# Routed experts as plain fp32 products, and one pass of the shared expert moved to the front

## The reference

```python
probs = softmax(xt @ w_router)                       # 16 experts
top_w, top_i = top_k(probs, 4); top_w = top_w / sum(top_w)
g = silu(einsum('td,edh->teh', xt, we1)) * einsum('td,edh->teh', xt, we3)   # H = 128
moe_out = einsum('teh,ehd->td', g * cw[:, :, None], we2)
shared = silu(xt @ ws1) * (xt @ ws3) @ ws2           # HS = 512
out = shared / 5 + moe_out * 4 / 5
x = x + gb * out
```

## Time and profile before

| | |
|---|---|
| median of 3 runs | 898.1 us (895.02 to 899.46) |
| profiled execution | 898.99 us, span 897.3 us, mean granted TensorE clock 0.917 |
| TensorE products / weight loads | 751.9 us (84%) / 469.8 us (52%) |
| VectorE | 662.9 us (74%) |
| ScalarE | 500.4 us (56%) |
| GpSimd | 268.4 us (30%) |

### The profile page before, as it was taken

How to read it: one execution, slowest core, us unless ns; L and a number is a source line. 1 busy time by engine, 2 the same in 40 slices (tenths; PEclk the granted TensorE clock), 3 DMA queues, 4 the chain that set the end, 5 groups by cost and what they waited for, 6 DMA issues and landing times. The chain is left out here.

```text
span 897.3 us, 15698 instructions
## 1 busy us (share of the span) xinstructions
PE 751.9 (84%) x5208; PEld 469.8 (52%) x5208; DVE 662.9 (74%) x1263; ACT 500.4 (56%) x939; POOL 268.4 (30%) x350
## 2 busy tenths in 40 slices
PE   8479699999999999999998968576788887888574
PEld 7246343444444444444444447465677776777453
DVE  7356888889998999999984377455777777776474
ACT  4221277678777877777776614434557775555111
POOL 7200013233222222233321121750007533420651
PEclk9777699999999999999999877899899998889799
DMA  6756014665544555344500112911337664543431
GB/s 195 183 117 202 18 32 95 180 162 145 148 128 135 154 153 152 82 127 112 133 26 4 50 39 66 333 71 57 109 112 240 220 186 144 159 148 99 145 93 58
DMA packets 78705, 112.37 MB, mean 125 GB/s; under 512 B 15780, under 2 KB 59364, under 8 KB 76516
## 3 DMA queue, kind: packets, MB, share of 16 engines
q1 hardware_dynamic: 68692, 81.67, 32.9%
q0 software_dynamic: 9280, 29.11, 9.5%
q10 hardware_dynamic: 656, 0.59, 0.4%
HBM read 59.92 MB, written 50.99 MB: 124 GB/s over the span
## 5 line engine op out<-in xcount | busy, mean ns | idle before, releaser
L750 ACT ACTIVATE probs<-psum 128x1024 f32<-128x1024 f32 (+3 forms) x384 | 289.8, 816 | 130.5 <-PE psum L935 128.0
L1156 DVE TENSOR_REDUCE max_parts<-psum 128x8 f32<-128x1024 f32 (+2 forms) x192 | 235.3, 1226 | 64.4 <-PE psum L909 60.8
L949 PE MATMUL psum<-probs,v_aug 128*32 128x512 f32 (+3 forms) x1536 | 168.1, 511 | 0.3 <-POOL probs L624 0.3
L935 PE MATMUL psum<-qs,ks 64*128 64x512 f32 (+3 forms) x768 | 157.3, 409 | 5.0 <-ACT probs L750 4.9
L624 POOL TENSOR_SCALAR_AFFINE_SELECT probs<-probs 128x512 f32<-128x512 f32 x128 | 81.6, 637 | 266.9 <-ACT probs L750 266.9
L935 PEld LDWEIGHTS psum<-qs,ks 64*128 64x128 f32 x768 | 73.4, 189 | 130.9 <-ACT probs L750 112.5
L1163 DVE TENSOR_REDUCE max_parts<-psum 128x1 f32<-128x512 f32 x192 | 130.7, 681 | 0.0
L909 PE MATMUL psum<-km,qs 64*128 64x128 f32 (+2 forms) x704 | 93.7, 338 | 34.9 <-DMA km<-k_parts 24.5
L1530 PE MATMUL psum<-w_all,km 128*128 x564 | 104.5, 326 | 10.6 <-issue 8.1
L1530 PEld LDWEIGHTS psum<-w_all,km 128*128 128x128 f32 x564 | 85.0, 214 | 18.8 <-issue 14.6
L1372 POOL DMA_INDIRECT probs<-y_sorted,posi x64 | 62.2, 972 | 106.7 <-DMA y_sorted<-xn 51.8
(11 more groups left out here) (204 smaller groups left out, 1008.7 us busy)
## 6 DMA issues: line engine op xcount, KB each, us to landing
km<-x_sorted SPq DMA_DIRECT2D x94, 128.0 KB, 2.4
y_sorted<-xn SPq DMA_DIRECT2D x94, 128.0 KB
km<-k_parts SPq DMA_DIRECT2D x62, 160.0 KB
x_sorted<-g_rows POOLq DMA_DIRECT2D x6, 1536.0 KB, 10.1
y_sums<-g_sign SPq DMA_DIRECT2D x32, 256.0 KB, 5.2
qs<-q_parts SPq DMA_DIRECT2D x62, 128.0 KB
ks<-k_parts SPq DMA_DIRECT2D x64, 64.0 KB
w_all<-in_L_ffn_we_dram SPq DMA_DIRECT2D x16, 256.0 KB, 6.0
```

The source lines that it names most:

```text
L750: act.activation(probs[s % (LAG + 1)][:, 2 * hh:2 * hh + 2, off:TT], psum[:, 2 * hh:2 * hh + 2, off:TT], ACT.Exp, scale=SCALE).then_inc(p_ ...
L935: last = pe.matmul(bank[2 * hh + hp][:, off:TT], ks[buf][rows, c * P:(c + 1) * P], qs[buf][rows, hh, half * TT + off:(half + 1) * TT], sta ...
L949: last = pe.matmul(bank[sum_bank][32 * h:32 * h + 32, off:TT], v_aug[:, group, c, :], probs[s % (LAG + 1)][:, h, off:TT], start=(c == 0), ...
L1156: dve.tensor_reduce(out=max_parts[:, :, h0:h1, slice(*tiles), slot], in_=psum[:, wide_bank:wide_bank + 2, :].rearrange("p a (s w) -> p (a ...
```

## The change

What it does:

- w_all holds the experts' weights once, as fp32. The splits of weights (ScalarE and VectorE in the lead), of x (VectorE) and of g (ScalarE and VectorE) are gone. A tile has two up products and one down product, in plain fp32.
- VectorE copies the turned g (`turned_out`) and all of y (`products_out`).
- The tile loop is reordered: TensorE up_rows(i), turned_rows(i+2), down_rows(i-2), turned_g(i-1); ScalarE silu(i), shifted_rows(i+2); VectorE product(i), products_out(i-2), turned_out(i-1). SyncE: load(i), store(i-5). up_rows waits for shifted_rows (t_read) instead of split_x.
- NY, the buffers for y, is 4 (3 before), NG, those for gathered rows, 4 (2 before). Tile buffers are their own and no longer parts of km, xn and probs; the first load no longer waits for the first pass.
- LEAD is 3: three passes stand before the tile loop, one behind it, which takes two combinations a step.

```diff
-        w_all = sb(moe, "w_all", [P, E, 2, WCOLS], F32R)
+        w_all = sb(moe, "w_all", [P, E, WCOLS], F32)
...
-        NX, NY, NG = 4, 3, 2
...
+        NX, NY, NG = 4, 4, 4
+        xg, xt = sb(moe, "x_rows", [P, NX, D], F32), sb(moe, "x_turned", [P, 2, D], F32)
+        tm, gt, yt = sb(moe, "tile_mid", [P, 2, P], F32), sb(moe, "tile_g", [P, 2, P], F32), sb(moe, "y_rows", [P, NY, D], F32)
+        acc, rows = sb(moe, "acc", [P, 2, D], F32), sb(moe, "rows", [P, NG, TOPK, D], F32)
...
-        AHEAD_T, BEHIND_Y, STORE_LAG = 3, 2, 8
+        AHEAD_T, STORE_LAG = 2, 5
...
-        LEAD = 2
+        LEAD = 3
...
                     if kk == 0:
                         sp.wait_ge(sorted_s[b], 16 * ROUTES)
-                    if k == 0:
-                        sp.wait_ge(up_full, 2 * NS)
                     if k >= NX:
                         sp.wait_ge(t_full, k - NX + 1)
                     sp.dma_start(xg[:, k % NX, :], xs[b][kk * P:(kk + 1) * P, :]).then_inc(x_in_s[k % NX], 16)
...
-                    if k % 2:
-                        sp.wait_ge(y_act, k // 2 + 1)
-                    else:
-                        sp.wait_ge(y_dve, k // 2 + 1)
+                    sp.wait_ge(y_copied, k + 1)
                     sp.dma_start(ys[b][kk * P:(kk + 1) * P, :], yt[:, k % NY, :]).then_inc(y_out_s[k % NY], 16)
...
-                        if t < 2:
-                            for expert in (2 * q, 2 * q + 1):
-                                act.wait_ge(w_in[expert // 4], 16 * 5)
-                                act.activation(w_all[:, expert, 0, :], w_all[:, expert, 1, :].bitcast(F32), ACT.Copy).then_inc(w_high, 1)
...
-                for i in range(-AHEAD_T, NTILE + BEHIND_Y):
-                    if 0 <= i + 1 < NTILE:
-                        silu(i + 1)
+                for i in range(-AHEAD_T, NTILE):
+                    if i >= 0:
+                        silu(i)
                     if i + AHEAD_T < NTILE:
                         shifted_rows(i + AHEAD_T)
-                    if 0 <= i < NTILE:
-                        high_rows(i)
-                    if i >= BEHIND_Y and (i - BEHIND_Y) % 2:
-                        products_out(i - BEHIND_Y)
...
-                        pe.wait_ge(w_low, E)
-                    pe.wait_ge(x_split, k + 1)
+                        pe.wait_ge(w_in, 16 * 5 * E // 4)
+                    pe.wait_ge(t_read, k + 1)
...
-                    for x, part in ((xh, 0), (xh, 1), (xl, 0)):
-                        for c in range(DC):
-                            last = pe.matmul(bank[U_BANKS[k % 2]][:, 0:2 * H], x[:, k % 2, c * P:(c + 1) * P],
-                                             w_all[:, bass.ds(expert[k], 1), part, c * 2 * H:(c + 1) * 2 * H].rearrange("p a n -> p (a n)"),
-                                             start=(n == 0), stop=(n == 5))
-                            n += 1
+                    for c in range(DC):
+                        last = pe.matmul(bank[U_BANKS[k % 2]][:, 0:2 * H], xt[:, k % 2, c * P:(c + 1) * P],
+                                         w_all[:, bass.ds(expert[k], 1), c * 2 * H:(c + 1) * 2 * H].rearrange("p a n -> p (a n)"),
+                                         start=(c == 0), stop=(c == DC - 1))
...
-                    pe.wait_ge(g_low, k + 1)
...
+                    pe.wait_ge(g_read, k + 1)
+                    if k >= 2:
+                        pe.wait_ge(y_copied, k - 1)
                     else:
-                        pe.wait_ge(y_dve, k // 2)
-                    for n, (g, part) in enumerate(((th, 0), (tl, 0), (th, 1))):
-                        last = pe.matmul(bank[Y_BANKS[k % 2]][:, 0:D], g[:, k % 2, :],
-                                         w_all[:, bass.ds(expert[k], 1), part, W13:WCOLS].rearrange("p a n -> p (a n)"),
-                                         start=(n == 0), stop=(n == 2))
-                    last.then_inc(y_full, 1)
+                        pe.wait_ge(shared_read, 2 * LEAD)
+                    pe.matmul(bank[Y_BANKS[k % 2]][:, 0:D], gt[:, k % 2, :],
+                              w_all[:, bass.ds(expert[k], 1), W13:WCOLS].rearrange("p a n -> p (a n)"),
+                              start=True, stop=True).then_inc(y_full, 1)
...
-                for i in range(-AHEAD_T, NTILE + BEHIND_Y):
-                    if 0 <= i + 1 < NTILE:
-                        up_rows(i + 1)
+                for i in range(-AHEAD_T, NTILE + 2):
+                    if 0 <= i < NTILE:
+                        up_rows(i)
                     if i + AHEAD_T < NTILE:
                         turned_rows(i + AHEAD_T)
-                    if i >= BEHIND_Y:
-                        down_rows(i - BEHIND_Y)
-                    if 0 <= i < NTILE:
-                        turned_g(i)
+                    if i >= 2:
+                        down_rows(i - 2)
+                    if 1 <= i <= NTILE:
+                        turned_g(i - 1)
...
-                        if t < 2:
-                            for expert in (2 * q, 2 * q + 1):
-                                dve.wait_ge(w_high, expert + 1)
-                                dve.tensor_tensor(out=w_all[:, expert, 1, :], in0=w_all[:, expert, 1, :].bitcast(F32),
-                                                  in1=w_all[:, expert, 0, :].bitcast(F32), op=ALU.subtract).then_inc(w_low, 1)
-                        elif t >= LEAD:
+                        if t >= LEAD:
...
-                def low_rows(k):
-                    dve.wait_ge(g_high, k + 1)
-                    dve.tensor_tensor(out=tl[:, k % 2, :], in0=bank[G_BANK][:, 0:P], in1=th[:, k % 2, :].bitcast(F32),
-                                      op=ALU.subtract).then_inc(g_low, 1)
+                def turned_out(k):
+                    dve.wait_ge(g_full, k + 1)
+                    if k >= 2:
+                        dve.wait_ge(y_full, k - 1)
+                    dve.tensor_copy(gt[:, k % 2, :], bank[G_BANK][:, 0:P]).then_inc(g_read, 1)
...
+                for i in range(NTILE + 2):
+                    if i < NTILE:
+                        product(i)
+                    if i >= 2:
+                        products_out(i - 2)
+                    if 1 <= i <= NTILE:
+                        turned_out(i - 1)
```

More of the change, by code:

```diff
@@ L1273, in block_kernel @@
         g_hi, g_lo = [km[k][:, DC * T:DC * T + TT] for k in (0, 2)]
-        xh, xl = [km[0][:, k * TT:(k + 1) * TT].rearrange("p (a n) -> p a n", a=2) for k in (0, 1)]
-        th, tl = [km[0][:, 2 * TT + k * 2 * P:2 * TT + (k + 1) * 2 * P].rearrange("p (a n) -> p a n", a=2) for k in (0, 1)]
-        NX, NY, NG = 4, 3, 2
[L1278 to L1286, removed]
+        NX, NY, NG = 4, 4, 4
+        xg, xt = sb(moe, "x_rows", [P, NX, D], F32), sb(moe, "x_turned", [P, 2, D], F32)
+        tm, gt, yt = sb(moe, "tile_mid", [P, 2, P], F32), sb(moe, "tile_g", [P, 2, P], F32), sb(moe, "y_rows", [P, NY, D], F32)
+        acc, rows = sb(moe, "acc", [P, 2, D], F32), sb(moe, "rows", [P, NG, TOPK, D], F32)
+        w_in = sem("experts_loaded")
         up_full, silu_done, mult_done = sem("up_full"), sem("silu_done"), sem("mult_done")
@@ L1293, in block_kernel @@
         y_out_s = [sem(f"tile_out_{k}") for k in range(NY)]
[L1294 to L1297, removed]
+        t_full, t_read, u_full, t_silu, t_mult, g_full, g_read, y_full, y_copied = [sem(n) for n in (
+            "tile_turned", "tile_shifted", "tile_up", "tile_silu", "tile_mult", "tile_g_turned", "tile_g_read", "tile_down", "tile_y_copied")]
         rows_in_s, combined, o_out = [sem(f"rows_gathered_{k}") for k in range(NG)], sem("combined"), sem("out_written")
         X_BANKS, U_BANKS, G_BANK, RANK_BANK, Y_BANKS = (0, 1), (2, 3), 4, 5, (6, 7)
-        AHEAD_T, BEHIND_Y, STORE_LAG = 3, 2, 8
+        AHEAD_T, STORE_LAG = 2, 5
         RANK_AT, FIRST_COMBINE = 14, TILES + 8
-        LEAD = 2
+        LEAD = 3
         def stored(eng, tiles):
@@ L1317, in _ @@
                             at = c * 2 * H + w * H
-                            sp.dma_start(w_all[:, es, 1, at:at + H].bitcast(F32),
-                                         src[es, c * P:(c + 1) * P, :].rearrange("e p h -> p e h")).then_inc(w_in[q], 16)
-                    sp.dma_start(w_all[:, es, 1, W13:WCOLS].bitcast(F32), we2_in[es].rearrange("e h d -> h e d")).then_inc(w_in[q], 16)
+                            sp.dma_start(w_all[:, es, at:at + H], src[es, c * P:(c + 1) * P, :].rearrange("e p h -> p e h")).then_inc(w_in, 16)
+                    sp.dma_start(w_all[:, es, W13:WCOLS], we2_in[es].rearrange("e h d -> h e d")).then_inc(w_in, 16)
                 def load(k):
@@ L1412, in shifted_rows @@
                     if k >= 2:
-                        act.wait_ge(x_split, k - 1)
+                        act.wait_ge(u_full, k - 1)
                     for c in range(DC):
-                        last = act.activation(ht[:, k % 2, c * P:(c + 1) * P], bank[X_BANKS[k % 2]][:, c * P:(c + 1) * P], ACT.Identity,
```

(30 more changed lines are left out.)

20 lines of the change are left out of this document (4 added, 16 removed).

## The result

Changed kernel: 912.93 us median of six runs (911.73 to 918.16), against 894.88 us of the kernel before in the same comparison (six runs, 891.68 to 899.46). The ratio is 1.0196 with a 95% interval of 1.016 to 1.0232: slower. Single executions of a kernel can fall into a slower state at a lower clock, and a ratio here compares the fast ones alone while a median takes all, so the ratio need not be the quotient of two medians.

The account below looks back on a forecast made before the run. The store-to-load loop in SyncE's queue was to bound the tiles. Span 897.3 + 17.9 (move) - 5.6 (weights) - 2.0 (first tile) + 1.6 (tiles) = 909.2, then + 1.7 - 0.9 = 910.0 us; range 899 to 929.

Parts of the forecast that it names:

- the loop: Tile stage: store, load, landing, turn and copy of y bound two tiles at 3.93 us, 1.97 each; stage 208.7 us.
- the move: One dense pass from tail to lead: +26.96 us in front, 9.1 back behind, net +17.9.
- The tail's sum: Tail, first of the last gathers to the end: gathers 40 us plus landing, combination and last outputs, 55.7 against 64.8.
- The weights' wait: First lead pass: ScalarE's wait for weights goes, 4.5 us, and 1.3 of clock; -5.6 taken, pass 27.4 long.
- The first turn: Start of the tiles: a sign of being right was the first turn of a tile at about 636.
- The lead's other passes: Lead: a dense pass priced at 26.96 us by the second pass of the kernel before.
- Rival B: Tiles while gathers run: loads land after 3.4 us, two tiles take 5.0; +16 us, 926; chance 0.15.
- Combinations: Tile stage: eight combinations of rows delay the copy of y and cost clock, 2.0 us each, 16 in all.
- Rival A: Tile stage: no loop, TensorE's 1.74 us a tile bounds; stage 190.5 us, total 891.8; chance 0.09.
- row and rule: TensorE's tile products: trace rows give plain fp32 0.07 us more a tile, a count of passes 0.42; rows followed.

Follow-up runs that it names:

- third group: Changed kernel, each edit alone (store lag 8; two passes in front) and both, beside the kernel before on one chip without standstills; changed kernel 915.18 us, ratio 1.0222.
- lag-8 kernel: Store lag 8 instead of 5 on the changed kernel, nothing else: 882.09 us, ratio 0.984 to the kernel before, on the chip without standstills.
- first two groups: Comparisons on two other chips, with standstills while GpSimd scatters: medians 957 to 997 us apart from a store lag of 4; kernel before 965.25 and 975.57.
- kernel with both edits: Store lag 8 and two passes in front, on the changed kernel: 870.52 us, ratio 0.9699 without standstills; 965.78 and 957.6 us with them.

## Why the prediction was right

The forecast was 910.0 from a before of 898.1, 1.3% slower; 912.93 and 1.96% came, inside the range. What was forecast is a difference of +11.9 us, and +18.05 came; that the two times lie only 2.9 apart is in part luck, since the kernel before took 3.2 us less in the comparison. Without attention, the third group's trace has the lead at 85.1 us against 63.9 (+21.2, forecast 19.4), the tiles at +5.7 (1.6), the way from the last tile to the gathers at +0.5 (0) and the tail at -8.4 (-9.1): +19.0 in sum. Every term erred a little towards too fast, the tiles most. Both mechanisms, the loop and the move, are as forecast. Step by step:

- The move. Forecast +26.96 - 9.1 = +17.9; the third group has +27 and -9.6 by stages, 11.6 to 15.4 in medians. Right, and a little large. The tail's sum of 55.7 from first gather to end was 56.1: the gathers waited for nothing but their own issue and took 40.7 us where 40 was put, and the last down products ran at half the clock (0.50 from 907 to 912) as supposed:

```profile
POOL rows L1357 <- issue: 9.4, 31, 0.3
...
907.25 2.07 PE L1453 MATMUL psum<-w_hi,km 128*128 128x256 f32 x8 [6.93 <-DVE km L1543]
```

- The weights' wait, -5.6: the first pass fell from 33.0 to 28.5, -4.5. Its idle time is the 7.5 us of every other pass, so the wait is wholly gone; what is left over 27.4 is time of the products, at a mean clock of 0.88. The first turn was to come at about 636 and came at 638.0, that near only because attention was 3.9 us shorter.
- The lead's other passes: 27 each forecast, 29.2 and 29.8 in this trace. This term was too small by 5 us in this trace, of which about 4 are this run's chance. The forecast held the clock to be settled by the code; the earlier trace rows had shown 0.94 for a pass once, and one row is no spread.
- The loop. The chain was put at 3.93 us for two tiles; 4.0 came. The tile stage was put at 208.7 and took 213.2, 212.8 in the third group. Undisturbed (tiles 40 to 52) four tiles took 7.8 to 8.2 as forecast, but 8.2 to 9.2 while GpSimd's scatters ran (tiles 24 to 40), where landing kept a median of 2.2 us and single loads took up to 3.3. Rival B came true in a small form where it was placed, at the gathers: the loads issued from 751 to 775 landed after 2.7 to 5.1 us, median 3.1, and tiles 52 to 60 took 9.9 and 13.1 us per four (9.7 and 11.7 in the third group), 4 to 5 us more than forecast.
- Combinations behind that: 8.7 to 10.5 us for four tiles (9.9 forecast).
- Rival A was worked out too small. It had 190.5 us for the stage without the loop, and the lag-8 kernel took 179.4: 1.69 us a tile, not 1.74, and four tiles with a combination 8.2 to 8.5 instead of 9.4. The forecast let TensorE lose each combination's stall of 2.4 us; it lost 1.5; why less isn't shown. So the loop costs 33 us and not 18: 11 because the stage without it is shorter, 4 because the stage with it is longer. By the forecast's account the loop and the move were worth the same, 18 us each; measured, the lag is worth twice as much.
- Where row and rule differed, on plain products, the rows held: one instruction of 128x256 columns every 0.22 us, up products of a tile (four) 1.03 us with drain. With six such instructions a tile's products take 1.3 us where the nine split ones took 1.27: less than a tenth more, and without the loop the tile became shorter. By the four passes that the Trainium skill's page FP8 and Floating Point Precision (TensorE Precision Notes) gives a true fp32 product, against three split products, they should have grown by a third. The plain product itself agrees with that count, as an estimate: two instructions of 0.217 us are four times the 0.107 of 256 columns at 2.4 GHz. What the comparison missed is that the split products took 0.14 each.

So the new tile loop is the good half of this change, -28 us in the tile stage when the loop through the store is open (207.1 to 179.4). Plain products, the absent splits, the new order and the larger buffers are all in that figure, and no run separates them. The store lag takes away 33 us, more than the whole of it, and the moved pass costs another 12 to 15.

## What to carry to other kernels

When loads and stores share an in-order DMA queue, count the tiles between a store and the load issued behind it: with few, the whole way store wait, load, landing becomes a loop that bounds the kernel although every engine has slack, and here a lag longer by three tiles cost nothing. When a stage gets lighter, ask which of its prefetch distances were cut with it. Moving work to where it hides nothing pays its full length, while the place that it leaves gives back only what was not bound by something else.

## What the runs showed beyond the question

On the chips of the first two groups, ScalarE, VectorE and SyncE almost stopped while GpSimd issued its 32 indirect DMAs back to back, in every kernel traced there. The kernel with both edits, first a normal stretch and then one under the scatters, and who waited in it (688 to 726):

```profile
650.00:683.00 33.00, 30.23 (x173) 24.91 (x172) 20.63 (x69) 16.16 (x47) 2.77 (x3) 1.00 0.42 132
688.00:722.00 34.00, 7.99 (x26) 5.75 (x24) 2.00 (x6) 2.17 (x6) 24.29 (x26) 0.64 0.34 120
```

```profile
ACT tile_mid L1404 <- remote: 29.9, 3, 13.2
...
DVE y_rows L1582 <- remote: 14.3, 2, 9.2
```

In 34 us six VectorE instructions ran; ScalarE waited up to 13.2 us and VectorE up to 9.2 for something that no instruction of the core explains ("remote"). The same stretch of the first trace runs at full pace (700 to 735 above, 22 POOL instructions in it). In the changed kernel and its versions with a store lag of 5 or 8, four tiles took 41 to 42 us there and the lead was 23 to 28 us longer; four more tiles at the start of the gathers took 21 to 23 us, and the tail was 14 to 18 us longer. Against the third group the medians are 68 and 78 us higher for the kernel before and 82 to 96 for the others. Neither edit touches this, and the cause is open: nothing in the profile names it, and no run tests it. It shifted ratios by up to 3% (0.9699 without, 0.9922 and 1.0011 with it), which is why kernels are only compared within a group.
